# The five engine programs of an attention and FFN block in another order

## The reference

```python
def block(x, ctx, mask, ...):                       # ctx: 2 x 77 x 256, 16 heads of 16
    q = layernorm(x) @ Wq + bq
    k, v = ctx @ Wk + bk, ctx @ Wv + bv
    att = (q . k) / 4 * mask - 1e10 * (1 - mask)    # per head, 1024 x 77
    x = x + softmax(att) @ v @ Wo + bo
    y = layernorm(x)                                # no gain or bias
    h = relu(y @ w1[0] + b1[0])                     # only expert 0 counts, 256 -> 1024
    y = y + h @ w2[0] + b2[0]                       # 1024 -> 256
    return x + layernorm(y) * gamma + beta
```

## Time and profile before

| | us |
|---|---|
| median of 3 runs | 226.63 (225.81 to 226.74) |
| the profiled execution | 226.6 |
| its span, first to last instruction | 224.8 |
| TensorE busy | 198.1 (88%) |
| VectorE busy | 148.7 (66%) |
| ScalarE busy | 119.8 (53%) |
| GpSimd busy | 80.8 (36%) |
| first matmul starts | 8.99 |

### The profile page before, as it was taken

One profiled execution on the slowest core, in us unless ns is written; L12 is line 12 of the kernel. 1 busy time (PEld: TensorE's weight loads), 2 busy tenths in 40 slices (PEclk: granted clock), 3 DMA queues, 4 the chain that ended last, 5 costly groups with the idle time before them and its releaser, 6 DMA issues.

```text
span 224.8 us, 3534 instructions
## 1 busy us (share of the span) xinstructions
PE 198.1 (88%) x1264; PEld 153.4 (68%) x1264; DVE 148.7 (66%) x345; ACT 119.8 (53%) x216; POOL 80.8 (36%) x87
## 2 busy tenths in 40 slices
PE   0399979869968699798999999999999999999991
PEld 0376565437535557475879696667998899988990
DVE  0999999753936957454487219249664397895774
ACT  3298525826757085757725648986024960159200
POOL 4367952710000100598230104932245453371121
PEclk9999999967999999999999999999999999999999
DMA  6994498790999953995002230202000011010012
GB/s 216 382 358 141 152 242 187 140 260 0 208 211 230 211 130 73 156 175 110 5 1 74 71 70 4 73 0 96 0 0 3 0 48 47 3 47 0 3 70 70
DMA packets 14267, 23.99 MB, mean 107 GB/s; under 512 B 1716, under 2 KB 5300, under 8 KB 14250
## 3 DMA queue, kind: packets, MB, share of 16 engines
q1 hardware_dynamic: 13274, 22.71, 40.6%
q10 hardware_dynamic: 976, 1.06, 1.6%
HBM read 16.56 MB, written 6.55 MB: 103 GB/s over the span
## 4 chain that ended last, share of the span: by engine, by line
PE 65%; DMA 18%; SPq 7%; ACT 3%; issue 3%; DVE 2%; ACTq 0%; POOLq 0%; POOL 0%
DMA Sq<-nmx 7%; PE W L765 7%; PE W L768 6%; PE W L766 6%; PE acc L701 5%; PE W L751 5%; PE W L752 5%; PE W L753 5%; PE T L689 5%; DMA wk<-in_L_xattn_Wk_dram 3%; DMA wo<-in_L_xattn_Wo_dram 3%; DMA Sq<-qD 3%; PE M L668 2%; PE W L710 2%; DMA Mq<-qD 2%
## 5 line engine op out<-in xcount | busy, mean ns | idle before, releaser
L865 ACT ACTIVATE PT<-T 77x512 f32<-77x512 f32 x64 | 36.0, 591 | 21.8 <-PE T L689 20.2
L1005 DVE TENSOR_REDUCE mx<-M 128x6 f32<-128x462 f32 (+1 forms) x48 | 26.7, 579 | 19.9 <-PE M L668 19.7
L765 PE MATMUL W<-w2h,hh 128*128 128x256 f32 x128 | 36.6, 286 | 0.4 <-DVE aTl L1023 0.4
L768 PE MATMUL W<-w2h,hl 128*128 128x256 f32 x128 | 36.1, 282 | 0.0
L766 PE MATMUL W<-w2l,hh 128*128 128x256 f32 x128 | 36.1, 282 | 0.0
L689 PE MATMUL T<-Sq,KS 128*77 128x512 f32 x64 | 25.6, 431 | 7.7 <-DMA Sq<-nmx 5.5
L1180 POOL TENSOR_TENSOR hl<-hr,hh 128x512 fp32r<-128x512 f32 x12 | 16.1, 1338 | 43.6 <-ACT hh L911 43.6
L907 ACT ACTIVATE hr<-W,cst 128x512 f32<-128x512 f32 x32 | 22.0, 687 | 16.6 <-PE W L753 15.5
L751 PE MATMUL W<-x2h,w1h 128*128 128x512 f32 x64 | 25.8, 403 | 0.0
L765 PEld LDWEIGHTS W<-w2h,hh 128*128 128x128 f32 x128 | 24.1, 189 | 1.7 <-issue 1.5
L752 PE MATMUL W<-x2l,w1h 128*128 128x512 f32 x64 | 25.2, 394 | 0.0
(11 more groups left out here) (122 smaller groups left out, 407.9 us busy)
## 6 DMA issues: line engine op xcount, KB each, us to landing
Sq<-qD SPq DMA_DIRECT2D x16, 256.0 KB
xin<-in_x_dram SPq DMA_DIRECT2D x4, 512.0 KB, 7.5
qD<-qh SPq DMA_DIRECT2D x8, 256.0 KB, 3.7
qD<-ql SPq DMA_DIRECT2D x8, 256.0 KB, 3.6
Sq<-qD SPq DMA_DIRECT2D x16, 128.0 KB
out_dram<-xn SPq DMA_DIRECT2D x6, 256.0 KB, 2.0
Mq<-qD SPq DMA_DIRECT2D x6, 192.0 KB, 4.8
w1raw<-in_L_ffn_w_dram SPq DMA_DIRECT2D x2, 512.0 KB, 11.3
```

The costliest lines, as they stand in the source:

```text
L765: e.matmul(y, hh[:, f, q:q + 128], w2h[:, f * E:(f + 1) * E], start=(f == 0), stop=False)
L768: i = e.matmul(y, hl[:, f, q:q + 128], w2h[:, f * E:(f + 1) * E], start=False, stop=(f == 7))
L865: e.activation(PT[:, m % 6, :], T[m % 2][0:TK, :], ACT.Exp).then_inc(exped, 1)
L1005: e.tensor_reduce(heads, M[(nth[step] - 1) % 2][:, 0:w * KP].rearrange("p (g h t) -> p g h t", g=1 if s < 2 else 2, t=KP)[:, :, :, 0:TK], ...
```

## The change

Only the numbers in `TIMES` differ, for all five engines. No step, buffer, wait or transfer is added or taken away. The new numbers were found by a search over orders whose model of the engines has VectorE and GpSimd hold each other up and times transfers by SBUF ports. What moves most:

- **GpSimd**: `xbias(0)`, `xbias(1)`, `splitwo`, `split(1,2)` and `split(1,3)` leave the first 45 us and come behind; `ksid(0)` and `ksid(1)` come first; `norm(3)` comes before `sslot(4)`.
- **VectorE**: `norm(2)`, `norm(3)`, `scale(2)`, `scale(3)` come earlier among the reductions, `keys(KS,...)` later, `bqr` and `consts` behind `norm(0)`; `scale2(0)`, `turn2(0)` and the first `low` steps earlier.
- **ScalarE**: the cast of Wo (`splitwo`) from in front of `st(0,0)` to behind `st(0,15)`; `split(2,0)` and `split(2,1)` in its earlier place; `qproj(3,0)` and `qproj(3,1)` earlier; `mxt(1,1)` before `st(1,5)`; `turn2(0)` and `ffn1(0,...)` in front of `st(1,12)` to `st(1,15)`.
- **TensorE**: `turn(3)` and `qproj(2,1)` before `st(0,0)`, `qproj(3,0)` and `qproj(3,1)` before `st(0,8)`; `proj(0)` before `st(1,6)`, `turn2(0)` behind `st(1,11)`, and five `ffn1(0,...)` between it and `st(1,15)`; one `ffn2(0,...)` comes before `st(2,4)`.
- **SP**: `qload(1,1)` before `quadq(0,2)`; `quadq(1,1)` and `quadm(1,1)` before `maskm(0)` and `qload(2,0)`; `quadq(2,0)` and `masks(0)` before `quadm(2,0)`; `late(1)` from in front of `quadm(1,2)` to behind `quadm(2,3)`; `qproj(3,0)`, `qproj(3,1)` and `qlow(3,...)` later, `statics` to the start.

The core of the diff, with the lists cut to the lines that the above speaks of:

```diff
 TIMES = {
     "PE": {
-        "turn": "11.5 / 19.6 / 27.5 / 43.1",
-        "qproj": "13.7 16.7 / 21.5 24.4 / 31.4 34.5 / 45.0 51.1",
...
-        "mxt": "30.8 37.2 / 47.9 56.0 / 71.6 79.5 / 96.9 121.8",
...
-        "proj": "60.8 / 93.4 / 136.3 / 167.7",
-        "turn2": "70.1 / 102.4 / 148.8 / 176.6",
-        "ffn1": ("74.2 75.6 77.4 80.0 81.6 83.9 88.5 92.0 / 105.2 118.6 122.5 123.8 126.1 129.4 131.2 134.7 / 153.1 156.4 "
-            "157.8 159.2 160.6 162.0 163.4 166.3 / 182.0 183.4 184.8 186.2 187.6 188.9 190.3 191.7"),
+        "turn": "11.9 / 20.9 / 27.1 / 33.2",
+        "qproj": "14.9 18.4 / 22.7 25.1 / 29.4 34.6 / 37.1 43.1",
...
+        "mxt": "32.3 39.9 / 48.1 55.6 / 73.4 81.0 / 99.7 123.4",
...
+        "proj": "58.1 / 100.4 / 140.8 / 166.1",
+        "turn2": "66.0 / 108.6 / 150.7 / 175.0",
+        "ffn1": ("69.0 71.3 74.3 75.9 77.3 78.9 81.4 84.2 / 112.9 116.5 117.9 119.5 122.0 125.1 126.7 128.1 / 153.5 154.9 "
+            "156.2 157.6 159.0 160.4 161.8 163.2 / 180.4 181.8 183.2 184.6 186.0 187.3 188.7 190.1"),
...
     "ACT": {
-        "qproj": "17.0 19.2 / 23.9 29.3 / 33.6 42.5 / 48.6 53.3",
...
-        "splitwo": "32.3",
-        "split": "17.6 22.7 23.3 34.2 35.4 43.1 46.7 49.2",
...
-        "turn2": "71.9 / 103.0 / 149.5 / 177.3",
+        "qproj": "17.8 23.1 / 24.9 27.3 / 33.5 37.5 / 44.1 45.2",
...
+        "splitwo": "52.6",
+        "split": "20.1 22.5 28.8 29.3 29.9 30.4 43.6 51.0",
...
+        "turn2": "66.7 / 109.3 / 151.3 / 175.7",
...
     "DVE": {
-        "norm": "4.6 / 10.7 / 19.3 / 36.3",
-        "scale": "9.1 / 16.9 / 24.3 / 41.2",
...
-        "scale2": "68.3 / 100.2 / 144.0 / 174.5",
...
-        "low": ("78.0 80.5 88.3 93.6 / 121.2 125.8 132.4 142.5 / 158.2 160.8 163.6 167.5 / 185.0 186.4 187.8 189.2 190.5 "
-            "191.9 193.3 195.0"),
+        "norm": "4.4 / 10.5 / 14.7 / 19.7",
+        "scale": "9.0 / 17.4 / 21.7 / 29.2",
...
+        "scale2": "64.5 / 107.0 / 147.3 / 172.5",
...
+        "low": ("73.3 77.3 81.3 84.4 / 118.1 120.9 126.7 133.4 / 157.5 159.9 162.1 164.9 / 183.4 184.8 187.2 187.8 189.3 "
+            "190.6 191.8 193.6"),
...
     "POOL": {
-        "norm": "7.2 / 13.3 / 21.8 / 38.8",
-        "xbias": "28.7 / 41.5 / 85.7 / 89.7",
-        "splitwo": "32.9",
-        "split": "19.2 24.6 26.6 40.1",
+        "norm": "6.7 / 13.9 / 16.8 / 21.8",
+        "xbias": "56.2 / 80.3 / 114.8 / 123.8",
+        "splitwo": "53.3",
+        "split": "23.8 26.4 54.5 59.1",
...
     "SP": {
-        "late": "29.8 59.3",
...
-        "maskm": "49.7 56.0",
-        "masks": "66.6 78.7",
...
-        "qload": "17.7 22.7 / 34.1 38.3 / 51.6 57.1 / 74.3 76.5",
-        "quadq": "26.0 28.7 37.2 42.9 / 47.4 53.8 58.2 62.0 / 75.4 77.6 83.4 87.8 / 102.6 109.1 113.4 123.9",
-        "quadm": "32.1 33.2 39.4 41.2 / 51.0 52.7 60.9 63.1 / 73.7 79.8 84.5 88.9 / 103.7 110.2 123.3 125.0",
+        "late": "38.4 96.1",
...
+        "maskm": "52.5 61.1",
+        "masks": "66.7 81.6",
...
+        "qload": "18.4 23.7 / 34.6 37.0 / 53.5 60.2 / 76.4 80.6",
+        "quadq": "25.6 28.4 40.1 43.8 / 47.9 51.0 59.2 62.6 / 65.8 79.1 87.5 94.7 / 101.1 107.1 114.8 127.4",
+        "quadm": "33.6 35.5 42.2 43.3 / 49.4 52.0 58.7 62.1 / 75.0 80.1 89.8 95.6 / 102.0 108.1 126.0 127.0",
...
```

## The result

The changed kernel takes 214.27 us, median of 4 runs (213.92 to 214.4); the kernel before, run beside it, 226.22 (225.75 to 226.74). The ratio is 0.9469, 95% interval 0.944 to 0.9498: 12.0 us faster, where 9.0 were forecast. The profiled execution took 213.92 us, its span 212.1.

What follows compares the result with a forecast made beforehand. TensorE's own work bounds the kernel, plus 9.0 us before, 5.0 after and 16.2 of losses. Terms left 7.2 us, a gain of 9.0: 226.6 to about 217.5 us; forecast's own range 213.5 to 221, 8 in 10 within 213 to 225.3.

Steps and rivals of the forecast that it cites:

- 9 to 38 us: First stage, paced by VectorE: 3.5 us comes in, 2.1 goes out; TensorE loss 1.7 us for 1.89.
- `smax(1,0,2)` and `st(0,8)`: 38 to 47 us: Wo's cast later and qload(1,1) earlier leave 0.5 us at each, 1.0 for 2.74.
- the clock: TensorE's fall to half clock behind the 2.53 us idle would likely not recur: loss 0 for 3.41 us.
- `st(1,0)`: Chunk 1's first maxima row: about 5.3 us to land against 3.8 of TensorE work, leaving 1.5 us for 2.24.
- `st(1,8)`: Chunk 1, 7.2 us of work ahead and quadm(1,2) no longer behind the broadcasts: wait 0 for 2.16 us.
- chain to `turn2(0)`: After proj(0): 4.8 us through GpSimd's power and scale2 against 3.9 of TensorE work, 0.9 us newly lost.
- broadcasts before `turn2(1)`: b2, gamma and beta, issued shortly before bias2(0), delay scale2(1) on VectorE: 1.0 us lost, bounds 0 and 4.
- `mxt(1,1)` (GpSimd's burst): GpSimd work moved to 53 to 60 us, some 6 us, charged nothing because VectorE has room there.
- ScalarE's block on Wo: ScalarE waiting for Wo until 36.6 us delayed exponentials, quadq(0,2) and the Mq load: the 2.53 us wait at 46.66.
- The estimate of 2.6 us on VectorE: At 53 to 60 us, by the shared-port rule, up to two hold-ups by GpSimd; 218 us if reaching proj(0).
- The rival: The waits only move: chunk 1's maxima rows still land late, near half the gain is lost, 221.5 us; 18%.
- The signs: Right: listed idles gone, last matmul by 211, full clock. Wrong: GpSimd on broadcasts past 105 us, new idle behind 110.

Runs made afterwards that it cites:

- e4: Changed kernel, three SP moves undone: maskm(0) ahead of quadm(1,0), qload(2,0) ahead of quadq(1,1), broadcasts ahead of quadm(1,2); 221.47 us, ratio 0.9916 to the kernel before.
- e11: Kernel before with one SP entry moved, qload(1,1) in front of quadq(0,2); 224.61 us, ratio 0.9947.
- e1: Kernel before with ScalarE's cast of Wo behind chunk 0's last exponential and GpSimd's subtraction behind xbias(1); 226.15 us, ratio 1.006.
- e8: Changed kernel with GpSimd's split(1,2), split(1,3), xbias(0) and xbias(1) back in the first 45 us; 216.0 us, ratio 0.9698 to the kernel before.
- e2: Kernel before with GpSimd's two splits, xbias(0) and xbias(1) moved out of the first 45 us; 226.53 us, ratio 1.0064.
- e3: Kernel before with SP's new order around chunk 1: its quads ahead of maskm(0) and qload(2,0), broadcasts behind chunk 2's loads; 240.26 us, ratio 1.0552.
- e10: Kernel before with the edits of e1, e2 and e3 together; 240.69 us, ratio 1.0702.
- e13: e12 with TensorE's smax(2,...,0) also moved behind st(1,7); 228.43 us, ratio 1.0253 to the kernel before.
- e12: Kernel before with e11's move, qload(2,0) in front of quadq(1,1), maskm(0) behind quadm(1,1), broadcasts left in place; 227.49 us, ratio 1.015.

## Why the prediction was right, and where it was off

The direction, the place of the gain (all of it before 110 us) and the mechanism (transfers that are on SP's queue earlier or with less in front of them, less idle, no fall of the clock) were right, and 214.27 lies in the range and in the forecast's own. The gain was under-estimated by 3 us. The total hides misses of both signs: the terms that were charged came out 5.4 us smaller together, and 1.9 us came where nothing was charged. Term by term, loss left as forecast and as measured:

| term | forecast | measured |
|---|---|---|
| 9 to 38 us | 1.7 | 0.88 |
| `smax(1,0,2)` and `st(0,8)` | 1.0 | 0 |
| the clock | 0 | 0 |
| `st(1,0)` | 1.5 | 0 |
| `st(1,4)` | 0.5 | 0 |
| `st(1,8)` | 0 | 0.73, and 0.23 right behind it |
| chain to `turn2(0)` | 0.9 | 0 |
| `st(2,4)` | 0.3 | 0 |
| broadcasts before `turn2(1)` | 1.0 | 0.70 |
| `mxt(1,1)` (GpSimd's burst) | 0 | 0.95 |
| small ones | 0.3 | 0.2 |
| sum | 7.2 | 3.7 |

- **`st(1,0)`, the largest miss.** I took 5.3 us from the turn to the landed row, between 3.5 and 7, and 3.8 us of work in between. Work was 4.5 us (50.35 to 54.86), and the row had landed by then, less than 3.3 us behind its issue at 51.60. So the work was sized 0.7 us too small and the way to the landed row at least 0.8 too long; how near it came to the 3.5 of the undisturbed case can't be seen, as nothing waited for it. e4, with one waiting entry put back in front of the 8 KB, shows the other end: 6.14 us.
- **`smax(1,0,2)` and `st(0,8)`.** The move of `qload(1,1)` was right as a cause; e11 shows that it alone takes the wait at `smax(1,0,2)` away. The step of the prediction that led from ScalarE's block on Wo over late exponentials to a late load was wrong: e1 took the block away and the wait stayed at 2.22 us, and e11 took it away with hardly an earlier issue, by putting 384 KB behind the load. e11 shows more: on the old order the wait only turns into one of 1.91 us at `st(0,8)`. That this one also went needs the rest of the new order, and which part of it isn't shown.
- **The start.** VectorE went from 27.91 to 26.08 us busy, though a norm came in. The mean of `scale` over the run fell from 670 to 452 ns, that of chunk 2 from 3.69 us for four to 1.38, and the loss to 0.88. e8 prices what left: 2.6 us. I had set what comes in against what goes out and seen no gain left.
- **The clock.** No fall, 3.41 us saved, as forecast.
- **The burst at 53 to 60.** This was charged nothing, on the argument that VectorE has room. It has, in the mean; but one reduction that TensorE waits for stood right behind the held-up subtraction. The two hold-ups cost VectorE 1.07 and 0.50 us (1.75 and 1.18 less 0.68 each), 1.6 us, and of it 0.95 reached TensorE at `mxt(1,1)` and some more at `st(1,8)`. The rule of the Trainium skill named in the prediction ("SBUF — State Buffer", on the shared port pair) agrees with these rows: each of the two instructions ended some 0.6 us behind the end of GpSimd's, about its own length. The estimate of 2.6 us on VectorE that the prediction made by it was 1 too much, since the second subtraction started when only 0.6 us of GpSimd's instruction was left. The prediction also let the 3.69 us of `scale` agree with that rule. It spoke of instructions with two SBUF inputs, and `scale` reads one tensor and a scalar per row; that `scale` too is held up is shown by e8 and e2 (3.71 and 5.33 us), why it is isn't.
- **`turn2(0)` and `st(1,8)`.** The chain from the end of `proj(0)` (64.6) to the end of `scale2(0)` took 4.7 us (4.8 forecast), by this line of VectorE's timeline:

```profile
67.88 1.38 DVE L1058 TENSOR_SCALAR xn<-xin,mv,rs 128x256 f32<-128x256 f32 x4
```

  `turn2(0)` starts at 69.71 and no wait stands in front of it: the 0.73 and 0.23 us idle at `st(1,8)`, which the sum had at 0, lie in the same stretch. Without them TensorE would have come at 68.75, while `scale2(0)` still ran. So the loss that was put at `turn2(0)` came at `st(1,8)`, and only once; that is read from the timeline, not tried.
- **Rivals.** The waits didn't just move, in the full order. In the partial orders tried on the kernel before (e2, e3, e10 to e13) they did: none was measurably faster, and e3 and e10 lost 12 to 15 us. The rival was right about pieces of the change and wrong about the whole. Which moves of the other engines' lists the rest of the gain needs, beyond what e4 and e8 price, stays open.
- **The signs.** Of those named for "right", the last matmul ends at 207.1, `scale` is under 500 ns and the clock never fell; the idle at `st(1,8)` is smaller but not gone. Two of those named for "wrong" came, and were small: GpSimd waited on the broadcasts until 105.45 us, and 0.70 us of idle stands behind 110 us.

## What to carry to other kernels

In a kernel whose engines run fixed lists, an entry of one list can be priced only together with where the others read what it brings: SP's moves around chunk 1 were worth about 7 us in the new order and cost 12 to 15 in the old one. Ask of a late load what was issued in front of it: `qload(1,1)` of e11, issued at about the same time with 384 KB fewer ahead, took 2 us less to land. When two waits lie in one stretch of the path, charge the longer, not both. Room on an engine "in the mean" says nothing of one instruction: look at which reduction stands right behind the one that is held up, and who waits for it.

## What the runs showed of the hardware that was not expected

A subtraction of 128x512 on VectorE with two SBUF inputs took 0.68 us alone and up to 1.75 beside one of GpSimd, and GpSimd's own rose from 1.27 to 1.76. The `scale` of 128x256, with one tensor read, rose too, from 1.37 us for four to 3.71 in e8.

An 8 KB load landed within 3.3 us of its issue with 384 KB issued in the 1.5 us before it. It took 5.25 us at 72.02 in e13, and 6.98 and 9.20 us in the kernel before, each time with 768 KB or more issued in the 2 to 4 us before.

In these runs the clock didn't follow the length of an idle stretch. It fell around idles of 1.65 us (e12, before `st(0,8)`, 0.59 from 47 to 51 us), 1.91 (e11, 0.72 in the same stretch) and 2.53 us (the kernel before, 0.50), and not behind 2.56 us at 35.98 in e8, where it stayed at 1.00, nor behind 2.24 and 2.16 us. What decides it stays open.
